# Quadrant matmuls for the last projection of a two-layer convolution and attention kernel, and a new order of its first 60 microseconds

## What is computed

```python
# layer 0
v = round(clip(gn(x), -1, 1) * 127) / 127 * 0.6        # gn: normalised over groups of 4 channels
fv = v + 0.1 * v ** 3                                  # on 3x3 patches, padded by 1
out_i = conv3x3(fv, g_pos[i] - g_neg[i])               # three planes i, 128 -> 128 channels
x = x + output_factor * sum of weighted clip(round(out_i * 0.01 * 256) / 256) + bias
# layer 1, z = gn(x), per image
q, k, v = Wq @ z, Wk @ z, Wv @ z                       # 128 -> 64 channels, 4096 pixels
num, den = exp(B) @ (exp(k) * v), exp(B) @ exp(k)      # 64 x 64
x = x + Wm @ (q * num / den)                           # 64 -> 128 channels: the mix
```

## Time and profile before

| | |
|---|---|
| median of 3 runs | 1563.71 us (1562.73 to 1565.27) |
| profiled execution | 1562.54 us, of which the span is 1560.5 us |
| TensorE busy | 1454.3 us (93%), 7792 matmul records |
| VectorE busy | 1393.6 us (89%) |
| ScalarE busy | 1155.7 us (74%) |
| GpSimd busy | 503.7 us (32%) |

### The profile page before, as it was taken

The page is one execution under the profiler, slowest core; times in us unless marked ns, Lnnn a source line. Parts: engine busy times, 40 slices in busy tenths (PEclk is TensorE's granted clock), DMA queues, the critical chain, the costliest instruction groups (busy, mean ns, idle before and its releaser), DMA issues.

```text
span 1560.5 us, 22719 instructions
## 1 busy us (share of the span) xinstructions
PE 1454.3 (93%) x7792; PEld 622.2 (40%) x7792; DVE 1393.6 (89%) x2182; ACT 1155.7 (74%) x1501; POOL 503.7 (32%) x506
## 2 busy tenths in 40 slices
PE   2599999999999999999999999999999999999985
PEld 1354434344443434444343443434344443434332
DVE  5869898998989899898989989898998989899767
ACT  4447778786877878787787878778786877875463
POOL 3111333232433333243333323333332433333312
PEclk9799999999999999999999999999999999999997
DMA  5011012313222231322223132222313222221222
GB/s 203 1 54 30 26 28 50 113 28 108 55 63 73 55 108 28 108 55 70 67 54 109 28 109 57 57 80 53 110 28 108 55 58 78 55 55 28 68 68 81
DMA packets 29173, 103.80 MB, mean 67 GB/s; under 512 B 4032, under 2 KB 4224, under 8 KB 29056
## 3 DMA queue, kind: packets, MB, share of 16 engines
q1 hardware_dynamic: 20416, 70.86, 12.3%
q0 software_dynamic: 8640, 31.46, 10.6%
HBM read 37.29 MB, written 33.55 MB: 45 GB/s over the span
## 4 chain that ended last, share of the span: by engine, by line
PE 74%; DVE 18%; issue 5%; POOL 1%; ACT 1%; DMA 1%; DVEq 0%; SPq 0%; POOLq 0%; ACTq 0%
PE A L486 14%; PE A L488 12%; PE A L487 12%; PE L L546 7%; PE B L486 7%; PE B L488 7%; PE B L487 7%; PE L L590 4%; PE L L577 3%; DVE duo L1068 1%; DVE uall L1150 1%; DVE A L1120 1%; DVE duo L1117 1%; DVE uall L1123 1%; DVE q L1040 1%
## 5 line engine op out<-in xcount | busy, mean ns | idle before, releaser
L486 PE MATMUL A<-T,WH 128*128 128x504 f16 (+1 forms) x1152 | 438.9, 381 | 1.0 <-ACT uall L780 1.0
L488 PE MATMUL A<-T,WL 128*128 128x504 f16 (+1 forms) x1152 | 437.3, 380 | 0.0
L487 PE MATMUL A<-T,WH 128*128 128x504 f16 (+1 forms) x1152 | 437.3, 380 | 0.0
L1436 POOL TENSOR_TENSOR T<-t,T 128x512 f16<-128x512 f32 x192 | 244.5, 1298 | 407.5 <-ACT T L702 407.5
L745 ACT ACTIVATE junk<-xr,shift 128x1024 f16<-128x1024 f32 x244 | 280.1, 1148 | 7.3 <-DVE xr L1153 0.7
L1410 POOL TENSOR_TENSOR zl<-z,zh 128x512 f16<-128x512 f32 x120 | 150.8, 1276 | 397.7 <-ACT zh L813 396.7
L486 PE MATMUL B<-T,WH 128*128 128x504 f16 (+1 forms) x576 | 221.4, 384 | 25.9 <-POOL T L1436 16.3
L488 PE MATMUL B<-T,WL 128*128 128x504 f16 (+1 forms) x576 | 220.7, 383 | 0.9 <-issue 0.9
L487 PE MATMUL B<-T,WH 128*128 128x504 f16 (+1 forms) x576 | 220.7, 383 | 0.0
L486 PEld LDWEIGHTS A<-T,WH 128*128 128x128 f16 x1152 | 115.1, 100 | 194.0 <-issue 81.3
L488 PEld LDWEIGHTS A<-T,WL 128*128 128x128 f16 x1152 | 112.7, 98 | 136.2
(11 more groups left out here) (174 smaller groups left out, 2462.5 us busy)
## 6 DMA issues: line engine op xcount, KB each, us to landing
xr<-in_x_dram SPq DMA_DIRECT2D x64, 512.0 KB, 5.8
out_dram<-xr SPq DMA_DIRECT2D x64, 512.0 KB, 2.7
xr<-shared POOLq DMA_DIRECT2D x60, 512.0 KB, 4.6
xr<-in_L_conv_g_pos_dram SPq DMA_DIRECT2D x3, 576.0 KB, 9.4
xr<-in_L_conv_g_neg_dram SPq DMA_DIRECT2D x3, 576.0 KB, 11.8
xr<-in_L_conv_Wm_dram SPq DMA_DIRECT2D x2, 32.0 KB, 9.2
xr<-in_L_conv_Wq_dram SPq DMA_DIRECT2D x1, 32.0 KB, 11.3
xr<-in_L_conv_Wk_dram SPq DMA_DIRECT2D x1, 32.0 KB, 11.1
```

The lines of the kernel that those rows point to most:

```text
L486: nc.tensor.matmul(to, wh, th, start=fresh and y == 1, stop=False, skip_group_check=True)
L487: nc.tensor.matmul(to, wh, tl, start=False, stop=False, skip_group_check=True)
L488: done = nc.tensor.matmul(to, wl, th, start=False, stop=y == 2, skip_group_check=True)
L1436: last = nc.gpsimd.tensor_tensor(low, t32[:, pair, :, :, :].rearrange("p t e w -> p (t e w)"), high, ALU.subtract)
```

## The change

The mix becomes eight matmuls of 64 rows by 64 columns and 256 pixels, in two parts of four, with a wait on `consts_made` ahead of the one on `o_ready` (`waits_apart`, line 313). GpSimd makes the first image's scale between weight differences 0 and 1, no longer makes the first image's second low rows, and makes weight difference 2 only when VectorE has finished `weight_sums(1)`. The second low rows are made by VectorE (`head_rows_low`), between `transform(0, 1)` and `weight_sums(1)`.

```diff
--- before.py
+++ after.py
@@ -584,10 +584,16 @@
 
             def mix(image, k, w):
 
-                pe.wait_ge(o_ready, nth(image, NG, k))
-                for h in range(2):
-                    half = slice(h * IC, (h + 1) * IC)
-                    last = nc.tensor.matmul(banks[w][h], wmf[half, :], rec[w][half, :], start=True, stop=True)
+                waits_apart(pe, (o_ready, nth(image, NG, k)))
+
+                for part in range(2):
+                    at = slice(part * QUART, (part + 1) * QUART)
+                    for r in range(2):
+                        rows = slice(r * IC, (r + 1) * IC)
+                        for c in range(2):
+                            cols = slice(c * IC, (c + 1) * IC)
+                            last = nc.tensor.matmul(banks[w][r][cols, at], wmf[rows, cols], rec[w][rows, at],
+                                                    start=True, stop=True)
                 last.then_inc(mix_ready, 1)
 
             def second_layer(image, c):
@@ -1083,6 +1089,17 @@
                 nc.vector.tensor_tensor(t32[:, 2, :, 0, :], ab[:, :, 1, :], ab[:, :, 0, :], ALU.add)
                 nc.vector.tensor_tensor(t32[:, 2, :, 1, :], ab[:, :, 1, :], ab[:, :, 0, :], ALU.subtract
                                         ).then_inc(t_ready, 1)
+
+            def head_rows_low(g):
+
+
+                for pair in range(3):
+                    dve.wait_ge(th_ready, NP * g + pair + 1)
+                    high, low = (T[:, part, pair, g * TILES:(g + 1) * TILES, :, :]
+                                 .rearrange("p t e w -> p (t e w)") for part in range(2))
+                    last = nc.vector.tensor_tensor(low, t32[:, pair, :, :, :].rearrange("p t e w -> p (t e w)"),
+                                                   high, ALU.subtract)
+                last.then_inc(tl_ready, 1)
 
             def mix_middle(p, n, images):
 
@@ -1342,6 +1359,7 @@
             for y in range(3):
                 low_weights(0, y)
             transform(0, 1, ())
+            head_rows_low(1)
             weight_sums(1)
             phases(dve, phase)
 
@@ -1478,11 +1496,11 @@
 
 
             weight_difference(0)
+            scale_x(0)
             weight_difference(1)
-            scale_x(0)
             rows_low(0, 0, 0)
+            pool.wait_ge(sums_made, 2)
             weight_difference(2)
-            rows_low(0, 0, 1)
             phases(pool, phase)
```

## The result

The changed kernel takes 1554.9 us (median of 5 runs, 1553.43 to 1556.29), the kernel before, over 5 runs, 1562.86 us (1561.2 to 1565.27). The ratio is 0.9948, with a 95% interval of 0.9936 to 0.9959: 8.1 us less (6.4 to 10.0). The forecast was 1555.4, range 1552.8 to 1560.0. The profiled execution of the changed kernel took 1553.43 us, with a span of 1551.7.

What follows compares the result with a forecast made beforehand. TensorE's queue was taken to bound the steady part, a chain through GpSimd, ScalarE, VectorE and weight turns the head. Gains of 2.55 + 2.3 + 2.7 - 1.65 + 2.4 = 8.3 us gave 1555.4 us from 1563.7, range 1552.8 to 1560.0.

Steps and rivals of the forecast that it cites:

- Part 1: Head: first scale made before weight difference 1, ready at 16.8 us, so plane 0's weight turns start 2.55 us earlier.
- Part 2: Head: weight difference 2 made later, so L1068 of the second transform takes 1.22 us, not 3.52; gain 2.3 us.
- Part 3: Head: second low rows on VectorE instead of GpSimd, first convolution matmul sooner after the transform; gain 2.7 us.
- What is late next: Head, plane 1: difference 2 delays cubic_f(0, 3) and low part 1, TensorE's second turn waits; 1.65 us given back.
- Part 4: Steady part: mix as eight small matmuls takes 1.03 us, not 1.07, like the sums stage; 2.4 us over 60 mixes.
- The sum: Whole kernel: 5.9 us gained in the head and 2.4 in the mixes, 8.3 us in all.
- rival C: Mix: quadrants sharing a row half run one behind the other, 1.3 us more per mix, 1635 us; chance 0.04.
- slower: Whole kernel: the chance that the changed kernel measures slower than before, put at 0.05.
- Rival A: Head: difference 2 gets in first and TensorE drops to its lower clock; only 5.2 us gained, 1558.5; chance 0.17.
- Rival B: First images: something unseen holds its date, the head's gain ends in a wait, only mixes count; 1561.3; chance 0.06.
- Rival D: Mix: each extra matmul costs 0.04 us that doesn't overlap, 0.24 us per mix, 1571.8 us; chance 0.02.

Runs made afterwards that it cites:

- the scale alone: The kernel before with only the first image's scale moved ahead of weight difference 1; one execution took 1559.05 us.
- the mix alone: The kernel before with only the new mix of eight matmuls; 1559.59 us against 1562.15, ratio 0.9985.
- the head alone: The changed kernel with the old mix of two matmuls; 1555.74 us against 1562.15 for the kernel before, ratio 0.9955.

## Why the prediction was right

**Part 1** (2.55 us forecast for the turns). Measured 3.0 and 2.3 us in the two profiles of the changed kernel, 2.4 in the scale alone. The second profile went as the step said. The first did not: the prediction missed that difference 0 can start just before L1030 of the statistics, which then stands still, so that the scale was ready 1.9 us later than 16.8. It made no difference, since difference 1 now started only after the scale and held up quantise(0, 0) (1.80 us) and no longer L963 (L957 before), for about as long. The same pair of starts went either way in the other runs: 2.64 us for L1030 in the mix alone, 0.23 in the head alone. Difference 0 starts when its load lands, so this isn't part of the change. From the turns to the second transform no step had counted a gain; it took 12.4 us before, 12.1 and 11.6 in the two profiles of the changed kernel.

**Part 2** (2.3 us): 3.52 to 1.23, and back with the wait taken out.

**Part 3** (2.7 us): from the transform to the first matmul 2.7 us, before 5.2. The first matmul was forecast at 42.0 and came at 41.42 and 41.59.

**What is late next** (1.65 us given back, plane 1 at 66.0). The step named the right wait and the right cause: difference 2 beside `cubic_f(0, 3)`, then low part 1. The wait was 2.53 us in one profile and 1.21 in the other, but this isn't what counts: it varies with how soon TensorE gets there, and that with the spell at its lower clock from 41 us on (clock 0.90 and 0.83 from 40 to 60 us, below). Plane 1 is set by VectorE's low part, at 64.97 and 65.15. The forecast was 0.8 to 1.0 us too late: the second transform started at 34.97 and 35.14, not at 35.7, and difference 2 ended at 49.1 and 49.3, not at 50.0. So the head gave 6.9 (6.7 in the second profile) where 5.9 was forecast. That difference 2 loses the start to quantise(0, 3) was the right choice between 1.65 and 2.75.

**Part 4** (2.4 us). The stage takes exactly the time of the sums stage. The gain is 0.035 us and not 0.04, which was two rows rounded to 0.01: 2.1 us.

**The sum.** Each step came out near its size, but that the median came out 0.5 us from the forecast is in part luck. The head gave up to 1.0 us more than forecast and the mixes 0.3 less, and the spells at the lower clock, below, move one execution against another by more than either. Two slips change nothing: 60 x 1.3 is 78 us in rival C, and the 0.05 for "slower" should be C's and D's 0.06.

**Rival A** has a true core, though its first half, difference 2 ahead of quantise(0, 3), came in no run in which it follows the sums. These are the granted clocks of four stretches (start:end, length, busy and count of each engine, clock, DMA share, GB/s), in the kernel before, the changed kernel and its second profile:

```profile
40.00:60.00 20.00, 10.45 (x40) 5.20 (x41) 16.57 (x24) 7.45 (x11) 5.03 (x4) 0.62 0.00 0
60.00:80.00 20.00, 14.19 (x64) 8.30 (x63) 15.24 (x24) 12.20 (x19) 2.94 (x3) 0.91 0.00 1
...
1475.00:1495.00 20.00, 16.48 (x87) 6.23 (x86) 13.12 (x15) 9.06 (x14) 5.65 (x5) 0.91 0.20 52
```

```profile
40.00:60.00 20.00, 14.18 (x67) 8.62 (x68) 15.78 (x24) 7.60 (x11) 2.75 (x1) 0.90 0.00 1
60.00:80.00 20.00, 16.07 (x79) 9.37 (x77) 14.68 (x27) 12.20 (x19) 4.09 (x5) 0.91 0.00 0
80.00:95.00 15.00, 13.01 (x65) 6.90 (x64) 10.21 (x20) 8.46 (x12) 2.81 (x6) 1.00 0.39 141
1475.00:1495.00 20.00, 16.48 (x94) 6.23 (x93) 6.63 (x11) 14.81 (x18) 3.13 (x3) 0.83 0.21 53
```

```profile
40.00:60.00 20.00, 15.32 (x65) 8.70 (x66) 15.78 (x24) 7.87 (x12) 2.75 (x1) 0.83 0.00 1
60.00:80.00 20.00, 16.17 (x73) 9.30 (x72) 13.60 (x23) 11.77 (x19) 3.39 (x3) 0.74 0.00 0
80.00:95.00 15.00, 13.01 (x58) 6.45 (x56) 10.99 (x20) 5.82 (x9) 1.25 (x4) 0.89 0.39 141
```

Behind the long stops ahead of plane 0 (11.46 us) and of plane 1 (3.93 and 3.83 us), and again behind one of 3.52 us in the last image, TensorE is at the lower of its two levels, 1.2 GHz, where a convolution matmul starts each 0.43 us and not each 0.22. The shorter stop of which the prediction asked went both ways: 2.53 us ahead of the turn at 54.94 had no such spell behind it (granted clock 1.00 from 45 to 64 us), 1.82 us in the head alone had one (0.50 from 57 to 63 us). These spells differ between two executions of the same kernel: from 60 to 80 us 0.91 and 0.74, from 80 to 95 us 1.00 and 0.89. In the first profile of the changed kernel the spells of the head were short and the one in the last image longer (0.83 for 0.91): 1.0 us of the 9.9 that it was ahead at 1414 us were gone at the end. In the second, the longer spell at plane 1 cost 1.1 us up to 81 us, and a third from 88 us on, at the matmuls of plane 2, another 1.7: of the 6.7 us at plane 1, 4.3 were there at the second image. That is the kind of loss rival A named, in one execution of the two. Such a third spell, between 85 and 89 us or at 137 to 138 us, came in six of the ten profiles with the new head or most of it, and in none of the three others. Whether that is the change's doing or chance, ten against three profiles don't settle; it stays open.

**Rival B** had a first image that holds its date: not so, in the first profile 7.5 us were there at the first matmul of the second image (140.87 against 148.35), and the head alone gave 7.0 us over its runs. **Rival C** fell with the runs in two other orders, and for a stronger reason than the one given. **Rival D**, each short matmul at a cost of its own, and with it the 60 cycles of the Trainium skill ("TensorEngine Tiling (Array Packing)", Instruction Overhead): eight matmuls take 1.03 us where two took 1.06. The page's remark is on matmuls of few columns; with 256 the trace bears no such cost, and what a matmul more does show is the 6.7 ns between two starts.

## What to carry to other kernels

Where an engine is moved out of another's way, look for the next instruction that it meets: here difference 2 left the transform and met the cubic. Two gains that add up at one point may share what lies behind it: parts 2 and 3 together moved the first matmul by 5.4 us and plane 1 by 3.8, and 2.1 of these either would have brought alone. So price a step at the last point where all engines meet, not at the first milestone that moves: beside the other parts the low rows moved the first matmul by 2.6 us and plane 1 by 0.4. A stage in the same kernel with the same shape and number of instructions priced the new mix to the nanosecond.

## What the runs showed that I had not expected

- TensorE's quadrants don't hold each other up in any of the three orders tried: 1.027, 1.040 and 1.047 us for the same eight fp32 matmuls, and the first matmul of the last quadrant starts 20 to 40 ns after the very first.
- A VectorE instruction on four columns, with one tensor operand, took 2.50 to 2.66 us where it began between 0.03 us ahead of and 0.13 us behind a GpSimd subtraction of 1152 columns (six of the thirteen profiles), and 0.23 us where it began 0.11 us or more ahead of it (the other seven).
- quantise, with one int16 input in place of two operands, is held up as well (1.80 us for 0.43).
- At about 950 us, where by the code the second pass of the loop over four images begins, TensorE stops once or twice, for 0.9 to 1.4 us, without waiting for anything that the profile shows. In the timeline of the kernel before:

```profile
951.57 0.39 PE L486 MATMUL B<-T,WH 128*128 128x512 f16 x1 [1.15 <-issue]
...
954.38 0.39 PE L488 MATMUL B<-T,WL 128*128 128x504 f16 x1 [0.91 <-issue]
```

In all thirteen profiles the image in which this lies took 1.8 to 2.8 us longer than its neighbours, the kernel before among them (93.15 us for 90.74). In seven of them a part of this is a wait of 1.2 to 1.4 us for the statistics (L1030), some 25 us after the first stop. What makes the engine stop there the runs don't show.
